# A four-layer graph network on one core: relation counts summed on VectorE before one TensorE product, and attention gathers in groups of three columns

## What is computed

```python
x = layernorm(x + GCN(x))          # layer 0: one weight, symmetric degree norm
x = layernorm(x + SAGE2(x))        # layer 1: two mean-aggregating layers
x = layernorm(x + GAT(x))          # layer 2: RMS norm, 1024 -> 256, attention, 256 -> 1024
x = layernorm(x + gated_RGCN(x))   # layer 3: one weight matrix per edge type
```

```python
msg = xl[src] + xr[dst]                       # rows of 256 = 4 heads of 64
act = where(msg > 0, msg, 0.2 * msg)
e = einsum('ehd,hd->eh', act, att)            # one logit per edge and head
```

```python
for r in range(8):
    mask = edge_type == r
    sums = segment_sum(x[src] * mask, dst)
    cnt  = segment_sum(mask, dst)
    out += (sums / maximum(cnt, 1)) @ weight[r]
```

## Time and profile before

| | |
|---|---|
| median of 3 runs | 3855.83 us (3855.02 to 3870.96) |
| profiled execution, its own time | 3865.32 us |
| its span, first to last instruction | 3863.6 us |
| mean granted TensorE clock | 0.958 of 2.4 GHz |
| PE busy | 3556.5 us, 92% of the span |
| VectorE busy | 1811.1 us, 47% |
| POOL busy | 1232.8 us, 32% |
| ACT busy | 894.8 us, 23% |
| chain that ended last, shares | PE 69%, POOL 9%, DMA 8%, VectorE 5%, issue 5%, ACT 4% |

### The profile page before, as it was taken

The page is one execution under the profiler, slowest core; times in us unless marked ns, Lnnn a source line. Parts: engine busy times, 40 slices in busy tenths (PEclk is TensorE's granted clock), DMA queues, the critical chain, the costliest instruction groups (busy, mean ns, idle before and its releaser), DMA issues.

```text
span 3863.6 us, 55257 instructions
## 1 busy us (share of the span) xinstructions
PE 3556.5 (92%) x23017; PEld 3075.3 (80%) x23017; DVE 1811.1 (47%) x3965; ACT 894.8 (23%) x1339; POOL 1232.8 (32%) x947
## 2 busy tenths in 40 slices
PE   5998078999999799999999798999999999999988
PEld 4665068999999799977878686777778888888888
DVE  7863254222332343444443687755543333333466
ACT  0111023111110212212111783422212222222224
POOL 2677533322333037777777443000000000000021
PEclk8899589999999899999999899999999999999999
DMA  8588762565422444444443565523412222222233
GB/s 286 141 260 253 244 190 65 120 155 116 117 63 50 151 123 144 144 150 137 148 138 106 226 236 189 188 92 134 145 45 77 77 76 77 77 77 66 67 99 103
DMA packets 261671, 517.16 MB, mean 134 GB/s; under 512 B 85563, under 2 KB 134706, under 8 KB 259402
## 3 DMA queue, kind: packets, MB, share of 16 engines
q1 hardware_dynamic: 136310, 383.90, 29.5%
q0 software_dynamic: 74080, 52.74, 8.5%
q10 hardware_dynamic: 51030, 77.00, 5.7%
HBM read 335.88 MB, written 177.63 MB: 133 GB/s over the span
## 4 chain that ended last, share of the span: by engine, by line
PE 69%; POOL 9%; DMA 8%; DVE 5%; issue 5%; ACT 4%; SPq 0%; ACTq 0%; POOLq 0%; DVEq 0%
PE ps L372 43%; PE ps L699 15%; DMA EM<-ee,adr 3%; POOL gr L2061 3%; POOL EM L2049 3%; PE ps L462 3%; DMA T<-cnt,adr 2%; POOL gl L2061 2%; ACT pb L1820 2%; PE ps L585 2%; PE ps L586 2%; PE ps L587 2%; DVE eqj L854 1%; DVE eqj L851 1%; DMA slab<-T 1%
## 5 line engine op out<-in xcount | busy, mean ns | idle before, releaser
L699 PE MATMUL ps<-mh,whl 128*128 128x384 f32 (+2 forms) x2560 | 559.8, 309 | 20.6 <-DVE gs L1347 14.4
L372 PE MATMUL ps<-wb,xth 128*128 128x256 f32 (+1 forms) x2560 | 460.5, 282 | 7.2 <-DVE xtl L1028 5.2
L699 PEld LDWEIGHTS ps<-mh,whl 128*128 128x128 f32 x2560 | 432.2, 190 | 21.0 <-issue 14.5
L2022 POOL DMA_INDIRECT TR<-cnt,adr x167 | 272.1, 1629 | 533.9 <-DMA TR<-cnt,adr 502.6
L2099 POOL TENSOR_TENSOR graw<-graw,rsb 128x1280 f32<-128x1280 f32 (+1 forms) x2 | 6.2, 3088 | 1232.0 <-DMA graw<-GD 1232.0
L372 PEld LDWEIGHTS ps<-wb,xth 128*128 128x128 f32 (+1 forms) x2560 | 389.1, 186 | 8.2 <-DVE xtl L1028 5.4
L699 PE MATMUL ps<-ml,whl 128*128 128x384 f32 (+2 forms) x1280 | 393.9, 308 | 0.0
L372 PE MATMUL ps<-wb,xtl 128*128 128x256 f32 (+1 forms) x1280 | 358.4, 280 | 0.0
L372 PE MATMUL ps<-a,yy 128*128 128x384 f16 (+4 forms) x2560 | 344.1, 297 | 5.2 <-DVE yy L1359 5.2
L372 PE MATMUL ps<-a,xhb 128*128 128x384 f16 (+5 forms) x1280 | 341.1, 296 | 0.0
L372 PE MATMUL ps<-a,xob 128*128 128x384 f16 (+5 forms) x1280 | 339.8, 296 | 0.0
(11 more groups left out here) (291 smaller groups left out, 7013.4 us busy)
## 6 DMA issues: line engine op xcount, KB each, us to landing
TR<-zero_w SPq DMA_DIRECT2D x80, 625.0 KB, 4.3
wraw<-in_L_gnn_weight SPq DMA_DIRECT2D x64, 512.0 KB, 3.3
EM<-neg SPq DMA_DIRECT2D x10, 2500.0 KB, 22.2
ar<-TR SPq DMA_DIRECT2D x72, 320.0 KB
eb<-EM SPq DMA_DIRECT2D x9, 2500.0 KB, 9.1
ar<-TR SPq DMA_DIRECT2D x72, 305.0 KB
UD<-ue ACTq DMA_DIRECT2D x72, 256.0 KB, 3.1
uu<-UD SPq DMA_DIRECT2D x36, 512.0 KB, 6.2
```

Of the source, the lines that this page charges most:

```text
L372: i = pe.matmul(ap, l, r, start=(q == 0), stop=(q == len(pairs) - 1))
L699: ins = pe.matmul(ps[:, 0:cn], l, r, start=(q == 0), stop=(q == len(pairs) - 1))
L2022: return pool.indirect_dma_start(out=flat, out_offset=bass.IndirectOffsetOnAxis(ap=adr[:, n, t:t + 1], axis=0), in_=cnt[:, n, t:t + 1], in ...
```

## The change

1. **Counts.** For the halves n = 1 to 15 VectorE adds the ten row tiles of `a16` in fp16 into one tile `asum` (`sum_counts`), in three parts set behind the adds of o = 4, 5 and 6 of the half before: one instruction on a pair of tiles after tile 3 is there, two on pairs after tile 7, three on single tiles after tile 9. PE multiplies that one tile with the ones, one product per chunk. Half 0 stays as it was. For the halves 1 to 7 the count is moved from ahead of o = 0 to behind it. `tmp` is one buffer now in place of three, in `add_to_acc`, since `asum` takes the room.
2. **Gathers.** `NB` goes from 5 to 3 columns (56 groups), `gl` and `gr` have three buffers each (`NG`), `LAG` goes from 8 to 5. `behind` is scaled to groups of three.
3. **Scratch.** `zg` is moved away from `gr`, so the first `gr` gather no longer waits for `V("ed", 9)`; the first two slabs, which now share its room, wait for it.
4. **Exponential.** ACT runs one exponential of one column before its mark `s8`.

```diff
-NX, NL, NZ, NB, NPT, NA, LAG = 4, 4, 7, 5, 11, 3, 8
+NX, NL, NZ, NB, NPT, NA, LAG = 4, 4, 7, 3, 11, 3, 5
+NG, LAST_B = 3, (ET - 1) // NB
...
-    return min(max(int((t - 8) / 21.5), 0), 33)
+    return min(max(int((t - 6) / (4.3 * NB)), 0), LAST_B)
...
-        zg = at("zg", [128, NT, 256], F32, O + 139.5)
+        zg = at("zg", [128, 9, 256], F32, O + 102.5)
+        zg9 = at("zg9", [128, 1, 256], F32, 1)
...
-        gl = [at(f"gl{i}", [EP, NB, 256], F32, O + 129 + 5 * i) for i in range(2)]
-        gr = [at(f"gr{i}", [EP, NB, 256], F32, O + 139 + 5 * i) for i in range(2)]
+        gl = [at(f"gl{i}", [EP, NB, 256], F32, O + 129 + NB * i) for i in range(NG)]
+        gr = [at(f"gr{i}", [EP, NB, 256], F32, O + 139 + NB * i) for i in range(NG)]
...
+        asum = at("asum", [128, 2, 640], F16, 10)
...
             def count(n, h, av):
+                w.wait_ge(*V("ones_h"))
+                if n > 0:
+                    w.wait_ge(*V("asum", n))
                 for c, (o0, cn) in enumerate(HC[h]):
                     ps = psum.take("cnt", n, c)
-                    w.wait_ge(*V("ones_h"))
                     w.wait_ge(*psum.empty("cnt", n, c))
-                    sum_of(ps[:, 0:cn], [(ones_h[0:ROWS[k], :], av[0:ROWS[k], k, o0:o0 + cn])
-                                         for k in range(NT)]).then_inc(*P.tick("cnt", n, c))
+                    sum_of(ps[:, 0:cn], [(ones_h[:, :], asum[:, 0, o0:o0 + cn])] if n > 0 else
+                           [(ones_h[0:ROWS[k], :], av[0:ROWS[k], k, o0:o0 + cn]) for k in range(NT)]).then_inc(
+                        *P.tick("cnt", n, c))
...
-                count(n, h, av)
+                if n == 0:
+                    count(n, h, av)
                 w.wait_ge(*V("yo", rel))
                 for o in range(8):
+                    if n > 0 and o == 1:
+                        count(n, h, av)
...
+            def sum_counts(n, part):
+                if n == 16:
+                    return
+                u, av = HW[HALVES[n][0]], a16[n % 2]
+                w.wait_ge(*A("a16", n, (3, 7, 9)[part]))
+                w.wait_ge(*V.now())
+                if part == 0:
+                    w.wait_ge(*P("cnt", n - 1, 1))
+                    dve.tensor_tensor(asum[:, :, 0:u], av[:, 0:2, 0:u], av[:, 2:4, 0:u], ALU.add).then_inc(*V.tick())
+                elif part == 1:
+                    dve.tensor_tensor(asum[:, :, 0:u], asum[:, :, 0:u], av[:, 4:6, 0:u], ALU.add).then_inc(*V.tick())
+                    w.wait_ge(*V.now())
+                    dve.tensor_tensor(asum[:, :, 0:u], asum[:, :, 0:u], av[:, 6:8, 0:u], ALU.add).then_inc(*V.tick())
+                else:
+                    dve.tensor_tensor(asum[:, 0, 0:u], asum[:, 0, 0:u], asum[:, 1, 0:u], ALU.add).then_inc(*V.tick())
+                    w.wait_ge(*V.now())
+                    dve.tensor_tensor(asum[:, 0, 0:u], asum[:, 0, 0:u], av[:, 8, 0:u], ALU.add).then_inc(*V.tick())
+                    w.wait_ge(*V.now())
+                    dve.tensor_tensor(asum[0:98, 0, 0:u], asum[0:98, 0, 0:u], av[0:98, 9, 0:u], ALU.add).then_inc(
+                        *V.tick("asum", n))
...
-                    q = turn[0] % 3
+                    q = 0
...
                     add_to_acc(n, rel, h, o)
+                    if 3 < o < 7:
+                        sum_counts(n + 1, o - 4)
...
                 if q < 2:
-                    w.wait_ge(*P("xlr", 9))
+                    w.wait_ge(*V("ed", 9))
...
+            act.activation(t10[:, 0:1], onesf[:, 0:1], ACT.Exp).then_inc(*A.tick())
             A.at["s8",] = A.n
...
-                if t // NB >= 2:
-                    w.wait_ge(*V("ee", t // NB - 2))
+                if t // NB >= NG:
+                    w.wait_ge(*V("ee", t // NB - NG))
                 for to, table, row in ((gl, XL, 0), (gr, XR, 1)):
-                    if t == 0 and row == 1:
-                        w.wait_ge(*V("ed", 9))
```

More of the change, by code:

```diff
@@ L207, in program @@
         xd_first = [landed(f"xd_first{i}") for i in range(2)]
-        rows_in, em_put = [landed(f"rows_in{i}") for i in range(2)], landed("em_put")
+        rows_in, em_put = [landed(f"rows_in{i}") for i in range(NG)], landed("em_put")
         em_in, bd_in = [landed(f"em_in{i}") for i in range(2)], [landed(f"bd_in{i}") for i in range(2)]
@@ L1150, in vector @@
             w.wait_ge(*A("xd"))
+            for s in (*t_out, *t_in):
+                w.wait_ge(*s("last"))
             for i0, i1 in ((0, 5), (5, 9), (9, 10)):
                 r, m = ROWS[i0], i1 - i0
-                zf = zg[0:r, i0:i1, :].rearrange("p m f -> p (m f)")
+                zz_ = zg[0:r, i0:i1, :] if i1 < 10 else zg9[0:r, :, :]
+                zf = zz_.rearrange("p m f -> p (m f)")
                 w.wait_ge(*V.now())
                 for i in range(i0, i1):
-                    dve.tensor_tensor(zg[0:r, i, :].rearrange("p (h d) -> p h d", h=4), xlx[0:r, i, :, 0:64],
+                    dve.tensor_tensor(zz_[:, i - i0, :].rearrange("p (h d) -> p h d", h=4), xlx[0:r, i, :, 0:64],
                                       xrn[0:r, i, :].rearrange("p (h d) -> p h d", h=4), ALU.add).then_inc(*V.tick())
@@ L1160, in vector @@
                 w.wait_ge(*V.now())
-                dve.tensor_tensor(zg[0:r, i0:i1, :], zg[0:r, i0:i1, :], atb[0:r, None, :].broadcast_to([r, m, 256]),
-                                  ALU.mult).then_inc(*V.tick())
+                dve.tensor_tensor(zz_, zz_, atb[0:r, None, :].broadcast_to([r, m, 256]), ALU.mult).then_inc(*V.tick())
                 w.wait_ge(*V.now())
@@ L1167, in vector @@
                 dve.tensor_reduce(out=ed[0:r, i0:i1, :].rearrange("p m h -> p (m h)"),
-                                  in_=zg[0:r, i0:i1, :].rearrange("p m (h d) -> p (m h) d", h=4), axis=AX.X,
-                                  op=ALU.add).then_inc(*t)
+                                  in_=zz_.rearrange("p m (h d) -> p (m h) d", h=4), axis=AX.X, op=ALU.add).then_inc(*t)
             low2(2)
@@ L1191, in vector @@
             for b, t0 in enumerate(range(0, ET, NB)):
-                a, m = b % 2, min(NB, ET - t0)
+                a, m = b % NG, min(NB, ET - t0)
                 zl_, zr_, to = gl[a][:, 0:m, :], gr[a][:, 0:m, :], ee[:, t0:t0 + m, :].rearrange("p m h -> p (m h)")
@@ L1820, in exponentials @@
                 act.activation(pb[n][0:r, :], eb[a][0:r, :, h], ACT.Exp, bias=mx[0:r, a, h:h + 1]).then_inc(*A.tick("exp", i, h))
-            w.wait_ge(*V("ee", 33))
+            w.wait_ge(*V("ee", LAST_B))
             for h in range(3):
@@ L2054, in gpsimd @@
             for t in range(ET):
-                a, m = (t // NB) % 2, t % NB
-                if t // NB >= 2:
-                    w.wait_ge(*V("ee", t // NB - 2))
+                a, m = (t // NB) % NG, t % NB
+                if t // NB >= NG:
+                    w.wait_ge(*V("ee", t // NB - NG))
                 for to, table, row in ((gl, XL, 0), (gr, XR, 1)):
-                    if t == 0 and row == 1:
-                        w.wait_ge(*V("ed", 9))
                     pool.indirect_dma_start(
```

## The result

The changed kernel takes 3832.7 us (median of 6 runs, 3819.93 to 3836.49), the kernel before 3857.74 us in the same rounds; the medians are 25.0 us apart. The ratio, which is that of the means (3830.62 and 3861.45 us), is 0.992, with a 95% interval of 0.9897 to 0.9944, that is 31 us less (22 to 40). The forecast was 3817 us from 3855.83, 39 us less. The measured median lies 15.7 us above it and 1.7 us above the end of the wide range; 0.992 of 3855.83 would be 3825 us, 8 us above the forecast, inside the wide range and outside the narrow one.

The account below looks back on a forecast made before the run. Bound by PE in the relational layer and by racing POOL and PE streams in the gather stage; -35.9 + 4.1 - 7.1 = -38.9 us, giving 3817 us from 3855.83; narrow range 3815 to 3822, wide range 3807 to 3831.

Parts of the forecast that it names:

- What PE loses, 35.9 us: Relational layer, halves 1 to 15: one ones-product in place of ten per sum takes 35.9 us off PE.
- The adds, 1.4 and 0.8 us, and PE's wait of 4.1 us: VectorE's adds, priced at fp32 pace, stay hidden except behind half 0, where PE waits 4.1 us over build and half 1.
- Rival 3: Relational layer: adds cost less than the fp32 row, PE waits 0 to 2 us; 3813 to 3815 us, chance 0.25.
- The gather stage, -7.1 us: Attention-gather stage: two PE waits vanish, 7.1 us less; POOL's last put lands about 2126.5, PE's stream ends the stage.
- rival 1: The gather stage stays as long as it is, so only the counts gain: 3824 us, chance 0.2.
- four short instructions each on a VectorE that waits 395 us: Gather stage: the 22 more groups add four short VectorE instructions each, which cost nothing.
- The three puts that go ahead of the last gather, 4 us: POOL's stream: five puts in place of eight left for the tail; the three now done early cost 4 us.
- the missing wait of 8 us: POOL's stream: the first `gr` gather no longer waits 7.97 us; alone this gains nothing.
- the one for `wb_t`: Start of PE's `u` products: a 3.94 us wait for a bank goes, as its group now stands three columns earlier.
- the one for `ue`: PE in the gather stage: a 3.2 us wait goes, as VectorE reaches slab 44 some 12 us sooner.
- Scratch and exponential, 0: Two slabs made 220 us after `ed` cost nothing; the early exponential saves 0 and costs 0, with 0.7 us to spare.
- Slower by late logits: Rival, gather stage: logits come too late for the shorter lag and hold POOL every group; 3878 us at 1.2 us each, chance 0.03.

Follow-up runs that it names:

- c1: The whole change, but with groups of five columns in two buffers and a lag of eight as before, against the kernel before: 3824.59 us, ratio 0.9895.
- e1: Only the counts changed; gathers, scratch and exponential as in the kernel before: ratio 0.9919 against it.
- e5: The changed kernel itself run once more, nothing altered: 3830.33 us, ratio 0.9918 against the kernel before.
- e3: Kernel before with only the scratch moved and the early exponential; groups of five columns and lag of eight kept: ratio 0.9972.
- e2: The change without its counts part (gathers, scratch and exponential only), against the kernel before: ratio 1.0002.
- e10: The whole change with five columns and a lag of six in place of eight, on the disturbed chip: ratio 0.9841 against the kernel before.
- e8: The changed kernel with groups of four columns, two buffers and a lag of six, on the disturbed chip: ratio 0.9882 against the kernel before.
- e11: The changed kernel with groups of four columns, two buffers and a lag of six, on an undisturbed chip: 3817.24 us, ratio 0.989.

## Why the prediction was right, point by point

The counts were forecast rightly in mechanism and nearly in size, and they are the whole of the measured gain. The gather stage was forecast wrongly. In the profiles two misses cancel in part, 4.1 us too little gained in the stage and 2.3 us less of a wait in the counts; by the runs' times the forecast promised some 8 us too much, which is about what it gave the gathers.

**What PE loses, 35.9 us.** Right; every block shows it. From `nb` to the end the three profiles without the counts' change take 1722.0 to 1722.6 us, and the changed kernel and its repetition 1687.4 and 1687.7: 34.8 us less; 35.9 less the wait would be 34.1. With five columns it is 31 to 33 us less, as told at `c1`.

**The adds, 1.4 and 0.8 us, and PE's wait of 4.1 us.** The place and the mechanism were right: once, at the bank of o = 3 in half 1 (in `e1` and `e5` twice, 2.3 us together). The size was off, 1.8 us in place of 4.1, because the adds take 0.80 and 0.48 us and not the pace of fp32. The Trainium skill, "VectorE: DVE Perf Modes", section "What auto-detection actually checks", has a faster mode for a `tensor_tensor` of 16-bit tensors with unit step; the trace agrees, 0.83 us against 1.49, and the estimate by it, 1.4 us, came closer than my row. Rival 3 was right in this. VectorE starts the build 16.99 us after `low_up` starts (2447.32 to 2464.31), 5.3 us more than before; forecast were 7.4 by the row and 4.7 by the estimate from the rule.

**The gather stage, -7.1 us.** This is the step that failed, and rival 1 (the stage stays as long as it is, 31.8 us less in all) is what the medians say: 31 us for the whole, 31 for the counts alone, none for the gathers. I wrote that POOL would land its last put at about 2126.5 and PE's stream end the stage. PE's stream did end 7 us earlier, but POOL landed at 2137.0, since 22 more groups of shorter instructions hold its own for 11.4 us more. That "nothing" for "four short instructions each on a VectorE that waits 395 us" counted only what VectorE pays. The three puts that go ahead of the last gather, 4 us, and the missing wait of 8 us came as forecast. Of PE's two waits, the one for `wb_t` did go, but it is absent with the old groups too, in `e1`, so that part of the term was never the change's; the one for `ue` stayed, because slab 44 came 7.7 us sooner, not 12, and PE itself 7 us. One reading was off as well: the prediction let the last put of before land 2 us after the end of its issue, at 2139.6; the last puts of the changed kernel and of `e3` land 2.11 us after their start, which would be 2138.8, so the two streams ended about 1.2 us apart and not 0.4.

**Scratch and exponential, 0.** The exponential is 0 behind `nb`: from there to the end `e2` and `e3` take 1722.4 and 1722.0 us, 1722.6 before; no run has it without the scratch. The table load stands at 2131.11 with 1.28 us and its activation behind it with 0.20; the further drain of 1.38 us that the Trainium skill states in "ScalarE: Activation LUTs", section "What ACT_TABLE_LOAD costs", is not there, and was not before (load at 2151.75 for 1.28 us, exponentials from 2153.04). The scratch is not 0, in a way that the prediction only half saw: it took the 8 us off POOL's wait, called them worthless alone because PE's stream ended the stage, and `e3` shows that alone they bring 11 us, for PE's wait for `ue` hangs on POOL's stream through the groups and slabs.

**Slower by late logits.** POOL waited 2.0 us for logits, once, at the end. That rival did not come true; `e10`, which was to test it, was lost to the disturbed chip.

## What to carry to other kernels

Idle time of an engine is no licence to put instructions there: VectorE's two-operand instructions hold up POOL's indirect DMAs, so where POOL's stream is near the path, price each of them at what POOL loses (0.3 to 0.5 us per held instruction in the mean here), and look how their length fits POOL's step. When a change has several parts, run each by itself: here one part gave the whole gain, one gave 11 us and a third took them back. When two streams end a stage about 1 us apart, look whether one feeds the other before calling a gain on it nothing. And compare a stage from its own first instruction, in more than one profile: here the same gathers ended 5 us apart.

The best version of these runs is the change with groups of four columns, 3817.24 us, 0.989 (0.9872 to 0.9908); with five it is 0.9895 (0.9871 to 0.9919), not to be told from it. The changed kernel itself has 0.9920 and 0.9918; the intervals overlap, so that the better grouping is seen in the stage and not shown in the whole.

## What was not expected of the hardware

Beside the hold on POOL itself, its size: with four columns POOL's DMA instructions are busy for 14.5 us less than with five and 28.0 less than with three (one profile each; the two of the three-column kernel differ by 3.7), though VectorE does the same arithmetic in all. And one chip of those that these runs met ran the same kernels 6% longer (4111.58 against 3857.74 to 3867.62 us), and of `e8`'s 254 us over `e11`, the same kernel, all 254 lie between the first gather and `nb` (993.1 and 739.1 us). There TensorE stood for 122 us in pauses with no reason in the profile, waited 60 us for `ue`, and had the 1.2 GHz level for 238 of 992 us, 0.88 of 2.4 GHz in the mean, where `e11` has 1.00; the pauses began before the clock fell for the first time. Why, stays open.
